# Six layer norms of a pass split into two halves of two tiles, in a two-slot FP32 model on one core

## The chip, the cores and the metric

One core of a Trainium2 chip runs the whole program. The metric is the device time of one execution in microseconds. The engines are TensorE (PE; its weight loads are PEld), VectorE (DVE), ScalarE (ACT), GpSimd (POOL) and SyncE (SP), each with an instruction queue of its own that it works off in order. They wait for each other only by semaphores.

## The reference

A four-layer stack over `x` (64 batches x 64 tokens x 128 features) with a context (64 x 128 x 128): cross-attentions with 16 and 8 heads, a recurrent layer, mixtures of experts, linear, softmax and local attention, and a state-space layer. What matters here is the norm without weights that stands ahead of every block. The kernel takes the mean out of it through centred weight matrices, so that on the tokens only the multiply by 1/sqrt(v + eps) is left:

```python
def _layernorm(x, axis=-1, eps=1e-05):
    m = jnp.mean(x, axis=axis, keepdims=True)
    v = jnp.var(x, axis=axis, keepdims=True)
    return (x - m) / jnp.sqrt(v + eps)
...
    x = x + _L0_attn_ref(_layernorm(x, axis=-1), L0_attn_W_hg, L0_attn_W_out)
...
    x = x + _L1_xattn_ref(_layernorm(x, axis=-1), ctx_1024, L1_xattn_Wq, L1_xattn_bq, L1_xattn_Wk, L1_xattn_bk, L1_xattn_Wv, L1_xattn_bv)
    x = x + _L1_attn_ref(_layernorm(x, axis=-1), L1_attn_wqkv, L1_attn_wo)
...
    x = x + _L2_attn_ref(_layernorm(x, axis=-1), L2_attn_w_qkv, L2_attn_b_qkv, L2_attn_w_out, L2_attn_b_out)
...
    x = x + _L3_attn_ref(_layernorm(x, axis=-1), L3_attn_w_in, L3_attn_conv_w, L3_attn_conv_b, L3_attn_w_B, L3_attn_w_C, L3_attn_w_out)
    x = x + _L3_ffn_ref(_layernorm(x, axis=-1), L3_ffn_Wg, L3_ffn_bg, L3_ffn_W1, L3_ffn_b1, L3_ffn_W2, L3_ffn_b2)
```

These six calls are the norms `rnn`, `x1`, `lin`, `loc`, `ssm` and `m3` of the kernel.

## The kernel before

The 64 batches are worked in 4 passes of 2 slots; a slot holds 8 batches, that is 512 tokens as 4 tiles of 128 tokens (partitions) by 128 features. The two slots are two independent programs with buffers of their own (`X_0`, `X_1`, `P_0`, `ps_0` and so on), and every engine interleaves them: each engine's program is a Python generator per slot, a `yield` ends a segment, and `weave` takes the next segment from slot 0 or 1 by one bit of a long number in `ORDER` (2496 segments on TensorE, 2038 on VectorE, 610 on GpSimd). So the order on each engine is written out beforehand, and an engine stands wherever its next segment waits for a semaphore, whatever else would be ready.

A norm is a chain over three engines and back. The names here are those of six norms per pass: `rnn`, `x1`, `lin`, `loc`, `ssm`, `m3`, so 48 in all. VectorE adds a block's result to the residual `X` (four L1456 instructions of one tile each, or one L1438, L1447 of all four tiles), takes `bn_stats` of four tiles (L1358), `bn_aggr` of four tiles (L1363), adds epsilon for all four in one instruction (L1378, for `loc` L1694) and signals `var`. GpSimd raises 128x4 variances to the power -0.5 (L1851) and signals `rstd`. VectorE multiplies the four tiles, 128x512, by it (L1373, `P<-X,small`) and signals `tok`. TensorE turns the four tiles (L457, four transposes, `ps<-cst,P`), and ScalarE copies them out (L1087), upon which the block's matmuls begin. L1373 is also used for norms that the change leaves alone (`P<-P`, `P<-Z`, `ctok<-ctok`). Within VectorE each step that reads the one before waits for the semaphore `chain` (`link`).

Beside the chain, GpSimd multiplies the attention probabilities of the other slot (L1878), products of the gated experts (L1968), and context tiles of 128x1024 (L1888, L1892).

Of the kernel before, what the change touches and what calls it, by code (L numbers as in the profile page):

```python
# [13 lines left out]
D = 128  # L14
# [45 lines left out]
def offsets(table):  # L60
    at, out = 0, {}
    for name, n in table:
# [14 lines left out]
    pe=(2496, int(""  # L77
        "4120180e82000011000000000033dbffdf375f56bac10c1af4ddee629cc55cb06914148810afbdc018a1ca1dd3aea84c3e9c"
        "718588ed73ea800018bfd2ff8eeff53ec40001008e1d720e74051814070f83ff8382011c3a86cb5fd6febfbbc1c3fc3f6bec"
        "ccfc9476f7fbd7dee707114148a0a7def5401651c3ac0c754163eb71c58b2c5ae72000031bf767ff15fde3dc4a0c3e0ebb82"  # L80
        "246bffffc0003902b06a40100000e439f3ff8b6fd6eeffdff647fc30abfa6ee58a2955ed703911029140530ef3d502c48e0e"
        "baea85bfff7b7be0b144aacd402003e97fd1f15d1f4000129ddea1b801158affffe1a82e00e20000000896b8ff7faeb75f5f"
        "fc1860ae9bffefeffc1f85bf2f38ca502505053d3ced401660e33f2d482affffffffe07ffbdffffeefc192d91eeb2a041812"
        "dfb1ff19e1d41389fff30f", 16)),
    act=(1740, int(""
        "4401061400110000000337bffe4faf4fbbecfa82c43130cc0901c000424af78f68bde1856031e6e0e18fee19bfff58103014"
        "e974e32054b018c306405ee0ccfddff73fffee99f10e8fbf7be8b0cc090382010ab95a0f687de350c30cdaa00f1fecc9bffd"
        "d21ccbfaed022dbf00068fb40010001773393fdefffde7fefeef1a24256470cc024118020224f0efcd3fffb35f0081ed5070"
        "fa7f80df9800ecf5fc310055f1e58ff000000009cf3e7bbf67ffbb7ff5ff13e03e6e06c0840e02010cb62fe641bffffff5ff"
        "f4ffff5838af0bfd2213de037fa0178ff", 16)),  # L90
    dve=(2038, int(""
        "51c7388080000c0000007fdaef5f0ec569738a609769cf6c61853036fc5b143437e800f1a3a936bb996fc30e0c0ca2361f15"
        "7ef2dcdbdbb07d80514d3c18ec83bd80000620488fb961e400a5ff9c78fe3e7186a7f643cfffe78f03cfc5b1593fc3b5011d"
        "294e78078efc30e483c818c7c0d7bf35db6adf0bffef3703473b19000ad95848c200001f0081b5eebbbdeff07fc74975ccd7"
        "318648e83cfc3a16341a1b8b68a33294e77377e5fe8cf019946305faf5ddc0db283de6ef3038032e7e306dc5801800000e37"
        "0022eddcb9ffc441aa4fffeb5fe9e1ce79e037d928b46fc9e5011e88ce7b1913fbffffe1fffcffffe4f1b19c78c77f000eb3"
        "67fd", 16)),
    pool=(610, int(""
        "673400df30532b53182161b93a2fbb7378c7904c253ac34fc0ff53185609d43957dee378c7cb219c0e0dee3a2b53142131b5"
        "3af57f8db607c0b9807706bc935fa660ac0ae49ffff3be7d1d", 16)),  # L100
# [4 lines left out]
def weave(program, order):  # L105
# [5 lines left out]
    for k in range(count - 1, -1, -1):  # L111
# [11 lines left out]
          "x3.r", "ssm", "m3", "m3.oh", "x0"]  # L123
TURNS = ["lat", "rnn", "lora", "lora.c", "x1", "lin", "lin.y", "m1", "m1.y", "rms", "x2.c0", "x2.c1", "x2",
# [9 lines left out]
MANY = {"kv": KV, "var": VARS, "rstd": VARS, "tok": TOKENS, "zT_ps": TURNS, "zT": COPIES, "y_ps": SUMS, "x_biased": BIASED,  # L134
# [21 lines left out]
def build(nc, x, ctxin, ctok_in, fold, cols, weights, consts, out):  # L156
# [4 lines left out]
    with stack:  # L161
# [71 lines left out]
        def by_tile(ap):  # L233
            return ap.rearrange("p (t d) -> p t d", d=D)
# [157 lines left out]
        with nc.Block() as block:  # L392
# [61 lines left out]
            def _(pe):  # L454
# [4 lines left out]

                def turn_onehot(s, i, name, k):  # L460
# [212 lines left out]
                def rnn(s, i):  # L673
# [9 lines left out]
                    yield  # L683
                    pe.wait_ge(*on("tok", s, i, "rnn"))
                    turn(s, 0, N[s])
# [34 lines left out]

                def cross(s, i):
                    yield
                    pe.wait_ge(*on("tok", s, i, "x1"))
                    turn(s, 0, N[s])
                    yield
                    pe.wait_ge(*on("zT", s, i, "x1"))
# [1391 lines left out]
```

## Time and profile before

| | us |
|---|---|
| median of 3 runs | 2501.07 (2498.35 to 2501.4) |
| the profiled execution, its own time | 2500.71 |
| its span in the trace | 2498.9 |
| TensorE busy | 2348.2 (94%) |
| VectorE busy | 1479.4 (59%) |
| ScalarE busy | 1179.5 (47%) |
| GpSimd busy | 930.1 (37%) |

Busy time is the union of an engine's instruction durations; what is left of the span is idle. TensorE has 150.7 us of it. The number behind a wait's arrow is the idle time of an engine just before an instruction, and the arrow names the instruction whose signal ended it.

### The profile page before, as it was taken

How to read it: one execution, taken by the hardware profiler on the slowest of the kernel's cores; microseconds unless marked ns; L12 is line 12 of the kernel's file. 1: busy time of each engine (PE TensorE's matmuls, PEld its weight loads, DVE VectorE, ACT ScalarE, POOL GpSimd, SP SyncE). 2: the span in 40 equal slices, each digit the busy share in tenths (PEclk: the TensorE clock that was granted, in tenths of full speed). 3: DMA queues.
4: the chain of work that ended last, by engine and by line, in shares of the span. 5: the costliest groups of instructions: out<-in, count | busy, mean ns of one | idle time of the engine just before them, and what ended most of it. 6: DMA issues, size and time to landing. Idle time of an engine off the chain costs nothing.

```text
span 2498.9 us, 41865 instructions
## 1 busy us (share of the span) xinstructions
PE 2348.2 (94%) x16412; PEld 1565.1 (63%) x16412; DVE 1479.4 (59%) x4008; ACT 1179.5 (47%) x2994; POOL 930.1 (37%) x853
## 2 busy tenths in 40 slices
PE   8999999999999999999999999999999999999998
PEld 5666665656756665665666666566566666656665
DVE  5457566665575666665564566665565555764653
ACT  4554334455444534445554454445455435354543
POOL 5334253533233335434232344543322343544400
PEclk8999999999999999999999999999999999999999
DMA  5000000000000000000000000000000000000000
GB/s 232 1 1 2 1 9 6 14 1 18 1 1 10 1 1 10 9 10 9 9 1 9 1 1 9 1 9 10 13 1 1 5 1 1 1 1 1 1 1 9
DMA packets 6676, 26.56 MB, mean 11 GB/s; under 512 B 848, under 2 KB 848, under 8 KB 5840
## 3 DMA queue, kind: packets, MB, share of 16 engines
q1 hardware_dynamic: 6480, 23.89, 2.6%
q8 instruction: 130, 2.13, 0.4%
q14 instruction: 66, 0.54, 0.1%
HBM read 21.79 MB, written 2.10 MB: 10 GB/s over the span
## 4 chain that ended last, share of the span: by engine, by line
PE 71%; DVE 17%; ACT 4%; POOL 4%; issue 3%; DMA 0%; SPq 0%; DVEq 0%; POOLq 0%; ACTq 0%
PE ps L472 10%; PE ps L485 7%; PE ps L529 6%; PE ps L504 6%; PE ps L866 4%; PE ps L606 3%; PE ps L496 3%; PE ps L583 3%; PE ps L457 3%; PE ps L576 3%; PE ps L628 2%; PE ps L581 2%; PE ps L823 2%; PE ps L813 2%; PE ps L655 2%
## 5 line engine op out<-in xcount | busy, mean ns | idle before, releaser
L1878 POOL TENSOR_TENSOR P<-P,small 128x384 f32<-128x384 f32 x384 | 317.3, 849 | 551.5 <-DVE small L1398 551.0
L1112 ACT ACTIVATE P<-ps,small 128x192 f32<-128x192 f32 x768 | 314.3, 421 | 154.9 <-DVE small L1390 153.3
L1851 POOL TENSOR_TENSOR small<-small,mhalf 128x4 f32<-128x4 f32 x112 | 129.0, 1151 | 554.0 <-DVE small L1378 317.0
L485 PE MATMUL ps<-kvT,big 128*128 128x192 f32 x1536 | 314.3, 335 | 6.8 <-DVE big L1405 2.5
L485 PEld LDWEIGHTS ps<-kvT,big 128*128 128x128 f32 x1536 | 248.6, 191 | 89.2 <-issue 52.1
L1390 DVE TENSOR_REDUCE small<-ps 128x2 f32<-128x384 f32 x384 | 210.1, 551 | 107.9 <-PE ps L485 100.5
L472 PEld LDWEIGHTS ps<-wts,P 128*128 128x128 f32 x1920 | 231.5, 192 | 43.8 <-issue 30.0
L472 PE MATMUL ps<-wts,P 128*128 128x128 f32 x1920 | 249.0, 279 | 5.2 <-POOL P L1968 2.6
L1968 POOL TENSOR_TENSOR P<-T 128x512 f32<-128x512 f32 x96 | 126.6, 1319 | 206.6 <-ACT T L1259 107.7
L504 PEld LDWEIGHTS ps<-value,big 128*128 128x128 f32 x1536 | 178.2, 192 | 25.8 <-issue 20.4
L504 PE MATMUL ps<-value,big 128*128 128x128 f32 x1536 | 188.2, 278 | 0.0
L529 PE MATMUL ps<-kvT,score 128*128 128x512 f32 x384 | 181.1, 613 | 6.5 <-ACT kvT L1087 5.0
L496 PE MATMUL ps<-cst,P 128*128 128x128 f32 x1152 | 166.4, 278 | 18.5 <-POOL P L1878 9.0
L496 PEld LDWEIGHTS ps<-cst,P 128*128 128x128 f32 x1152 | 132.3, 143 | 50.2 <-issue 18.2
L1112 ACT ACTIVATION_READ_ACCUMULATOR P<-ps,small 128x1 f32 x768 | 157.0, 204 | 0.0
L1285 ACT ACTIVATE P<-ps,col 128x512 f32<-128x512 f32 x128 | 81.3, 684 | 132.6 <-PE ps L870 132.5
L606 PEld LDWEIGHTS ps<-Vbd,P 128*64 128x64 f32 x3072 | 98.0, 139 | 53.5 <-issue 31.8
L372 POOL TENSOR_TENSOR big<-big,cst 128x1024 f32<-128x1024 f32 x48 | 106.5, 2222 | 65.2 <-ACT big L1277 37.8
L1456 DVE SCALAR_TENSOR_TENSOR X<-ps,small,X 128x128 f32<-128x128 f32 x256 | 71.9, 343 | 99.4 <-PE ps L472 94.0
L529 PEld LDWEIGHTS ps<-kvT,score 128*128 128x128 f32 x384 | 70.3, 194 | 84.5 <-issue 74.3
L1595 DVE TENSOR_REDUCE small<-ps 128x8 f32<-128x512 f32 x128 | 87.6, 685 | 58.4 <-PE ps L628 58.2
L1129 ACT ACTIVATE big<-ps 128x512 f32<-128x512 f32 x96 | 57.3, 597 | 133.0 <-PE ps L496 132.7
(281 smaller groups left out, 4476.0 us busy)
## 6 DMA issues: line engine op xcount, KB each, us to landing
ctok<-ctok_dram SPq DMA_DIRECT2D x8, 512.0 KB, 3.7
ctxT<-ctx_dram SPq DMA_DIRECT2D x8, 512.0 KB, 3.6
wts<-weights_dram SPq DMA_DIRECT2D x1, 2530.0 KB, 24.1
wts<-weights_dram SPq DMA_DIRECT2D x1, 2189.0 KB, 17.8
X<-x_dram SPq DMA_DIRECT2D x8, 256.0 KB, 3.4
big<-fold_dram SPq DMA_DIRECT2D x2, 1024.0 KB, 9.1
out_dram<-X SPq DMA_DIRECT2D x8, 256.0 KB, 2.0
wts<-weights_dram SPq DMA_DIRECT2D x1, 1536.0 KB, 26.7
```

Of the source, the lines that this page charges most:

```text
L372: return engine.tensor_tensor(big[s][:, 1024 * (t % 2):1024 * (t % 2) + 1024].rearrange("p (b j t) -> p b j t", b=2, t=SEQ), src[:, 128 * ...
L472: m = pe.matmul(part(s, k, t), tile_of(src, t), w, start=first and t == 0 and c == 0, stop=last and t == TILES - 1 and c == len(pairs) - 1)
L485: m = pe.matmul(ps[s][:, at:at + KEYS], big[s][:, BANK * b + 128 * p:BANK * b + 128 * p + 128], kvT[s][:, keys_at(b):keys_at(b) + KEYS], s ...
L496: m = pe.transpose(part(s, k, p), probs(s, j)[:, PAIR * p + at:PAIR * p + at + 128], C("ident"))
L504: m = pe.matmul(part(s, 1, t), big[s][:, 1024 * t + 128 * k:1024 * t + 128 * k + 128], value[:, at:at + 128], start=(t == 0 and k == 0), s ...
L529: m = pe.matmul(bank(s, qp_bank(g, r) + k), score[:, 128 * block_of(h, nh):128 * block_of(h, nh) + 128], latents(s), start=True, stop=True)
L606: m = pe.matmul(ps[s][64 * bb:64 * bb + 64, at:at + 18], src(bb, j), Vbd[s][:, 18 * (8 * b + j):18 * (8 * b + j) + 18], start=True, stop=True)
L1112: m = act.activation(probs(s, b // 2)[:, to:to + KEYS], ps[s][:, at:at + KEYS], ACT.Exp, bias=small[s][:, 4 * e + p:4 * e + p + 1], accum_ ...
L1390: dve.tensor_reduce(small[s][:, at:at + 2], ps[s][:, BANK * k:BANK * k + 2 * KEYS].rearrange("p (c k) -> p c k", k=KEYS), AX.X, ALU.max, n ...
L1851: pool.tensor_tensor(rstd(s, name, n), variance(s, name, n), mhalf[:, 0:n], ALU.pow).then_inc(*sig("rstd", s))
L1878: m = pool.tensor_tensor(view, view, over(small[s][:, at:at + 2], 2, [128, 2, KEYS]), ALU.mult)
L1968: pool.tensor_tensor(P[s][:, 1024 + 512 * (k % 2):1536 + 512 * (k % 2)], tmp(s, k % 2), tmp(s, 2 + k % 2), ALU.mult)\
```

## The change

For the six norms the work of four tiles is cut into two halves of two tiles. VectorE takes `bn_stats` of tiles 0, 1 and 2, aggregates 0 and 1, takes `bn_stats` of tile 3, adds epsilon for tiles 0 and 1 and signals `var` a first time, then aggregates 2 and 3, adds epsilon and signals a second time. GpSimd does two powers of 128x2, VectorE two multiplies of 128x256, TensorE two pairs of transposes, each behind its own wait. The signal to ScalarE (`zT_ps`) comes after the second pair, as before after the fourth transpose, and ScalarE's copy and all that follows is the same. Matmuls, transposes and their shapes are the same in number. `ORDER` has new numbers for every engine but SyncE.

```diff
 ORDER = dict(
-    pe=(2496, int(""
-        "4120180e82000011000000000033dbffdf375f56bac10c1af4ddee629cc55cb06914148810afbdc018a1ca1dd3aea84c3e9c"
...
+    pe=(2544, int(""
+        "8088190ca078016400000000008cf3dff7b78abafb858d0d5f4edd05c51578c88a0c445069f7bea5b073a75c54160000f938"
...
+                def turn_halves(s, i, name, k, src):
+                    for h in range(2):
+                        yield
+                        pe.wait_ge(*on("tok", s, i, name if h else name + ".0"))
+                        for t in (2 * h, 2 * h + 1):
+                            m = pe.transpose(part(s, k, t), tile_of(src, t), C("ident"))
+                    m.then_inc(*sig("zT_ps", s))
...
                 def cross(s, i):
-                    yield
-                    pe.wait_ge(*on("tok", s, i, "x1"))
-                    turn(s, 0, N[s])
+                    yield from turn_halves(s, i, "x1", 0, N[s])
...
+                    stats(0)
+                    first = mark(stats(1))
+                    stats(2)
+                    dve.wait_ge(chain, first)
+                    aggregate(0)
+                    first = mark(aggregate(1))
+                    second = mark(stats(3))
+                    dve.wait_ge(chain, first)
+                    plus_eps(0)
+                    dve.wait_ge(chain, second)
+                    aggregate(2)
+                    link(aggregate(3))
+                    plus_eps(1)
+
+                def rescale_halves(s, i, name, dst, src):
+                    for h in range(2):
+                        yield
+                        dve.wait_ge(*on("rstd", s, i, name if h else name + ".0"))
+                        dve.tensor_tensor(by_tile(dst)[:, 2 * h:2 * h + 2, :], by_tile(src)[:, 2 * h:2 * h + 2, :],
+                                          over(rstd(s, name)[:, 2 * h:2 * h + 2], 2, [128, 2, D]), ALU.mult).then_inc(*sig("tok", s))
...
-                    yield from norm(s, i, "x1", res(s, i), N[s], weights_centred=True)
+                    yield from norm_halves(s, i, "x1")
...
+                def inverse_root_halves(s, i, name):
+                    for h in range(2):
+                        yield
+                        pool.wait_ge(*on("var", s, i, name if h else name + ".0"))
+                        pool.tensor_tensor(rstd(s, name)[:, 2 * h:2 * h + 2], variance(s, name)[:, 2 * h:2 * h + 2], mhalf[:, 0:2], ALU.pow)\
+                            .then_inc(*sig("rstd", s))
```

What the orders show at three places. The line numbers after the change are those of the new file: 472 are the transposes of a half, 487, 832 and 822 what 472, 823 and 813 were, 1909 what 1860 was, 2017 what 1968 was.

TensorE in pass 0, between the last matmuls of slot 1's `lora` block (`ps_1<-wts,T_1`) and the transposes of its norm `x1`; before:

```order
L472 MATMUL ps_1<-wts,T_1 128x128 x3
L823 MATMUL ps_0<-A_0,wts 128x512 [waits m1_t0,m1_ab0]
L813 MATMUL ps_0<-A_0,wts 128x512
L472 MATMUL ps_0<-wts,P_0 128x128 [waits m1_g0]
L472 MATMUL ps_0<-wts,P_0 128x128 x3
L823 MATMUL ps_0<-A_0,wts 128x512 [waits m1_t0,m1_ab0]
L813 MATMUL ps_0<-A_0,wts 128x512
L457 MATMUL ps_1<-cst,P_1 128x128 [waits tok1]
L457 MATMUL ps_1<-cst,P_1 128x128 x3
```

and after:

```order
L487 MATMUL ps_1<-wts,T_1 128x128 x3
L832 MATMUL ps_0<-A_0,wts 128x512 [waits m1_t0,m1_ab0]
L822 MATMUL ps_0<-A_0,wts 128x512
L487 MATMUL ps_0<-wts,P_0 128x128 [waits m1_acc0,m1_g0]
L487 MATMUL ps_0<-wts,P_0 128x128 x3
L832 MATMUL ps_0<-A_0,wts 128x512 [waits m1_t0,m1_ab0]
L822 MATMUL ps_0<-A_0,wts 128x512
L472 MATMUL ps_1<-cst,P_1 128x128 [waits tok1]
L472 MATMUL ps_1<-cst,P_1 128x128
L472 MATMUL ps_1<-cst,P_1 128x128 [waits tok1]
L472 MATMUL ps_1<-cst,P_1 128x128
```

The same eight matmuls of slot 0 (four of 512 columns, four of 128; the trace has two records of each FP32 matmul) lie ahead of the transposes; the second pair stands directly behind the first.

TensorE in pass 2, between slot 0's state-space output (`ps_0<-wts,P_0`) and the transposes of its norm `m3`; before:

```order
L472 MATMUL ps_0<-wts,P_0 128x128 x7
L581 MATMUL ps_1<-big_1,T_1 128x512 [waits pT_act1]
L583 MATMUL ps_1<-A_1,T_1 128x512
L584 MATMUL ps_1<-A_1,T_1 128x512
L504 MATMUL ps_1<-value2,big_1 128x128 [waits exped1]
L504 MATMUL ps_1<-value2,big_1 128x128 x7
L496 MATMUL ps_1<-cst,P_1 128x128 [waits p_ready1,mix_dve1,mix_act1]
L496 MATMUL ps_1<-cst,P_1 128x128 x3
L457 MATMUL ps_0<-cst,P_0 128x128 [waits tok0]
L457 MATMUL ps_0<-cst,P_0 128x128 x3
```

and after:

```order
L487 MATMUL ps_0<-wts,P_0 128x128 x7
L519 MATMUL ps_1<-value2,big_1 128x128 [waits exped1]
L519 MATMUL ps_1<-value2,big_1 128x128 x7
L511 MATMUL ps_1<-cst,P_1 128x128 [waits p_ready1,mix_dve1,mix_act1]
L511 MATMUL ps_1<-cst,P_1 128x128 x3
L511 MATMUL ps_1<-cst,P_1 128x128 [waits p_ready1]
L511 MATMUL ps_1<-cst,P_1 128x128 x3
L472 MATMUL ps_0<-cst,P_0 128x128 [waits tok0]
L472 MATMUL ps_0<-cst,P_0 128x128
L511 MATMUL ps_1<-cst,P_1 128x128 [waits pT_act1]
L511 MATMUL ps_1<-cst,P_1 128x128 x3
L472 MATMUL ps_0<-cst,P_0 128x128 [waits tok0]
```

Less of slot 1 lies ahead of the norm's transposes than before (the mixing matmuls L581 to L584 went ahead of slot 0's output), and four transposes of slot 1 lie between the two pairs.

VectorE in pass 0 at the norm `x1` of slot 1, from `bn_stats` on. Before, with its last step:

```order
L1358 BN_STATS small_1<-X_1_0 128x6 x3
L1363 BN_AGGR small_1<-small_1 128x2 [waits chain]
L1363 BN_AGGR small_1<-small_1 128x2 x3
L1378 TENSOR_SCALAR small_1<-small_1 128x4 [waits chain]
L1675 SCALAR_TENSOR_TENSOR T_0<-P_0,ps_0 128x512 [waits m1_g0,m1_t0]
L1373 TENSOR_TENSOR P_1<-X_1_0,small_1 128x512 [waits rstd1]
```

and after:

```order
L1383 BN_STATS small_1<-X_1_0 128x6 x2
L1386 BN_AGGR small_1<-small_1 128x2 [waits chain]
L1386 BN_AGGR small_1<-small_1 128x2
L1383 BN_STATS small_1<-X_1_0 128x6
L1389 TENSOR_SCALAR small_1<-small_1 128x2 [waits chain]
L1386 BN_AGGR small_1<-small_1 128x2 [waits chain]
L1386 BN_AGGR small_1<-small_1 128x2
L1389 TENSOR_SCALAR small_1<-small_1 128x2 [waits chain]
L1410 TENSOR_TENSOR P_1<-X_1_0,small_1 128x256 [waits rstd1] x2
L1718 SCALAR_TENSOR_TENSOR T_0<-P_0,ps_0 128x512 [waits m1_g0,m1_t0] x2
```

The experts' product of slot 0, which stood between epsilon and the multiply, now stands behind both multiplies.

## Rows read from the trace of the kernel before

**Rows 1.** The page's busy times, granted TensorE clock, and chain by engine.

```profile
PE 2348.2 (94%) x16412; PEld 1565.1 (63%) x16412; DVE 1479.4 (59%) x4008; ACT 1179.5 (47%) x2994; POOL 930.1 (37%) x853
...
PEclk8999999999999999999999999999999999999999
...
PE 71%; DVE 17%; ACT 4%; POOL 4%; issue 3%; DMA 0%; SPq 0%; DVEq 0%; POOLq 0%; ACTq 0%
```

**Rows 2.** TensorE's waits over the span: us in total, times, longest.

```profile
PE ps L457 <- DVE P L1373: 30.9, 42, 2.9
PE ps L496 <- POOL P L1878: 9.0, 14, 2.2
PE ps L472 <- DVE big L1470: 7.4, 5, 2.6
```

**Rows 3.** Timeline, norm `x1`, slot 1, pass 0: start, duration, engine, line, idle before.

```profile
309.09 0.87 DVE L1358 BATCH_NORM_STATS2 small<-X 128x6 f32<-128x128 f32 x4
...
309.37 1.05 PE L472 MATMUL ps<-wts,P 128*128 128x128 f32 x8
...
310.26 1.02 PE L823 MATMUL ps<-A,wts 128*128 128x512 f32 x2
...
311.12 1.02 PE L813 MATMUL ps<-A,wts 128*128 128x512 f32 x2
...
312.56 0.66 PE L457 MATMUL ps<-cst,P 128*128 128x128 f32 x4 [0.42 <-DVE P L1373]
```

**Rows 4.** Timeline, norm `ssm`, slot 1, pass 3, with nothing beside the chain.

```profile
2440.03 0.86 DVE L1358 BATCH_NORM_STATS2 small<-X 128x6 f32<-128x128 f32 x4
...
2440.93 0.38 DVE L1363 BATCH_NORM_AGGREGATE small<-small 128x2 f32<-128x6 f32 x4
2441.34 0.17 DVE L1378 TENSOR_SCALAR small<-small 128x4 f32<-128x4 f32 x1
2441.59 1.01 POOL L1851 TENSOR_TENSOR small<-small,mhalf 128x4 f32<-128x4 f32 x1 [4.40 <-DVE small L1378]
2442.63 0.69 DVE L1373 TENSOR_TENSOR P<-X,small 128x512 f32<-128x512 f32 x1 [1.12 <-POOL small L1851]
...
2443.38 0.66 PE L457 MATMUL ps<-cst,P 128*128 128x128 f32 x4 [1.16 <-DVE P L1373]
```

**Rows 5.** Timeline of TensorE, pass 3: the last of the 25 waits counted.

```profile
2450.37 0.66 PE L457 MATMUL ps<-cst,P 128*128 128x128 f32 x4 [0.25 <-DVE P L1373]
```

**Rows 6.** Groups by line and shape of GpSimd: shape, count, busy us, mean ns, idle before.

```profile
L1851 POOL TENSOR_TENSOR small<-small,mhalf 128x4 f32<-128x4 f32 x112 | 129.0, 1151 | 554.0 <-DVE small L1378 317.0 <-DVE small L1480 165.5 <-DVE small L1694 37.4
...
L1892 POOL TENSOR_TENSOR T<-T,col 128x1024 f32<-128x1024 f32 x16 | 34.7, 2166 | 1.2
...
L1892 POOL TENSOR_TENSOR T<-T,col 128x512 f32<-128x512 f32 x16 | 17.5, 1093 | 1.1
...
L1948 POOL TENSOR_TENSOR small<-small,mhalf 128x4 f32<-128x4 f32 x8 | 8.0, 1003 | 0.0
...
L1997 POOL MEMSET A<- 128x8 f32 x8 | 0.9, 114 | 0.0
```

**Rows 7.** Groups by line and shape of VectorE, same columns.

```profile
L1373 DVE TENSOR_TENSOR P<-X,small 128x512 f32<-128x512 f32 x48 | 48.4, 1008 | 22.4 <-POOL small L1851 22.1
...
L1585 DVE TENSOR_TENSOR kvT<-ps,small 128x128 f32<-128x128 f32 x96 | 27.9, 291 | 3.3
```

**Rows 8.** Timeline, pass 1: `m3` of slot 0 beside a GpSimd multiply.

```profile
1152.34 2.00 POOL L1888 TENSOR_TENSOR T<-ctok,col 128x1024 f32<-128x1024 f32 x1
...
1152.41 2.48 DVE L1373 TENSOR_TENSOR P<-X,small 128x512 f32<-128x512 f32 x1
...
1154.94 0.78 PE L457 MATMUL ps<-cst,P 128*128 128x128 f32 x4 [1.42 <-DVE P L1373]
```

**Rows 9.** Timeline, pass 2: a power on GpSimd, and a VectorE multiply beside it.

```profile
1450.33 1.01 POOL L1948 TENSOR_TENSOR small<-small,mhalf 128x4 f32<-128x4 f32 x1
...
1450.40 0.69 DVE L1373 TENSOR_TENSOR P<-Z,small 128x512 f32<-128x512 f32 x1 [0.31 <-POOL small L1851]
```

More of the change, by code:

```diff
@@ L123, with halves @@
           "x3.r", "ssm", "m3", "m3.oh", "x0"]
+HALVED = ["rnn", "x1", "lin", "loc", "ssm", "m3"]
+def halves(names):
+    return [m for n in names for m in ([n + ".0", n] if n in HALVED else [n])]
 TURNS = ["lat", "rnn", "lora", "lora.c", "x1", "lin", "lin.y", "m1", "m1.y", "rms", "x2.c0", "x2.c1", "x2",
@@ L1459, in rnn @@
                 def rnn(s, i):
-                    yield from norm(s, i, "rnn", res(s, i), N[s], weights_centred=True)
+                    yield from norm_halves(s, i, "rnn")
                     yield
@@ L1609, in linear @@
                 def linear(s, i):
-                    yield from norm(s, i, "lin", res(s, i), N[s], weights_centred=True)
+                    yield from norm_halves(s, i, "lin")
                     yield
@@ L1692, in local @@
                     yield
-                    moments(s, "loc", res(s, i))
-                    dve.tensor_scalar(variance(s, "loc"), mean_var(s, "loc")[:, :, 1], EPS5, None, ALU.add).then_inc(*sig("var", s))
+                    moments_halves(s, "loc", res(s, i))
                     link(dve.tensor_reduce(small[s][:, MEAN:MEAN + 8], ctxT[s][:, :].rearrange("p (b k) -> p b k", k=CTX), AX.X, ALU.add))
@@ L1697, in local @@
                        .then_inc(*sig("x3_sum", s))
-                    yield from rescale(s, i, "loc", N[s], res(s, i))
+                    yield from rescale_halves(s, i, "loc", N[s], res(s, i))
                     yield
@@ L1762, in ssm @@
                 def ssm(s, i):
-                    yield from norm(s, i, "ssm", res(s, i), N[s], weights_centred=True)
+                    yield from norm_halves(s, i, "ssm")
                     yield
@@ L1792, in moe3 @@
                 def moe3(s, i):
-                    yield from norm(s, i, "m3", res(s, i), N[s], weights_centred=True)
+                    yield from norm_halves(s, i, "m3")
                     yield
@@ L1925, in program @@
                         yield from heads(s, i, 1)
-                        yield from inverse_root(s, i, "rnn")
+                        yield from inverse_root_halves(s, i, "rnn")
                         yield
@@ L1978, in program @@
                         yield from heads(s, i, 2)
-                        yield from inverse_root(s, i, "loc")
+                        yield from inverse_root_halves(s, i, "loc")
                         yield
@@ L1992, in program @@
                         yield from inverse_root(s, i, "x3")
-                        yield from inverse_root(s, i, "ssm")
+                        yield from inverse_root_halves(s, i, "ssm")
                         yield
```

88 lines of the change are left out of this document (46 added, 42 removed).

## The prediction

> **What bounds the kernel now.** I read the page's busy times first, then TensorE's waits, then the timeline at single norms. TensorE is busy 2348.2 of 2498.9 us, and the chain that ended last runs 71% over TensorE and 17% over VectorE [rows 1]. The order changes no matmul, and the granted clock stands at 9 tenths or more in all slices after the first [rows 1]. So what can be won lies in TensorE's 150.7 us of idle time, and what can be lost is added to it. The largest single entry there is the wait of the transposes for the norm's multiply on VectorE: 30.9 us in 42 waits; the next, for the normalised probabilities, is 9.0 us [rows 2]. No other engine is near its limit (59%, 47%, 37%), so their own work counts only where TensorE waits for it.
>
> The 30.9 us aren't all of the six norms. Matching the 42 waits with the norms, in the order in which they stand on TensorE, 25 belong to the six norms, from 0.42 us at 312.56 [rows 3] to 0.25 us at 2450.37 [rows 5]; they add to 17.2 us. The other 17 waits, 13.7 us, are at norms that stay whole. At 23 of the 48 changed norms TensorE doesn't wait at all, since enough work of the other slot lies ahead.
>
> **The chain before.** Where nothing disturbs it [rows 4], from the first statistic: VectorE's moments end at 1.48 us, the power runs from 1.56 to 2.57, the multiply from 2.60 to 3.29, TensorE starts at 3.35. Four transposes at a spacing of 0.12 us (0.66 less the last one's 0.27 or so of latency, over three) end the chain at about 3.84 of TensorE's time.
>
> **The change, part by part.** *Statistics on VectorE.* Four of them span 0.86 us, four aggregates 0.38 [rows 4], so three statistics, two aggregates, one more statistic and an epsilon of 0.17 give the first `var` at about 1.2 us. Two aggregates and a second epsilon follow; the second `var` comes at about 1.5, as the only one did. The added instruction falls in time that was spent on `chain` waits.
>
> *The power.* The trace has no 128x2 power. Four columns take 1.00 us (1003 ns undisturbed; the mean of 1151 holds cases lengthened by a running VectorE multiply, [rows 6]), and two directly behind each other aren't faster (the second has no idle time before it and still takes 1003). Half of it is bounded from above by 1.00, if the cost belongs to the instruction. From below: a small memset of 8 columns takes 0.11, which I take as the fixed part, and half of the rest gives 0.56. GpSimd's multiplies speak for the lower end: 512 columns take 1093 ns, 1024 take 2166 [rows 6], twice as much, with next to nothing fixed. I take 0.60. Then the first power runs 1.28 to 1.88, the second 1.88 to 2.48 (by then the second `var` has been there for long). With 1.00 it would be 1.28 to 2.28 and 2.28 to 3.28.
>
> *The multiplies.* 128x512 takes 0.69 us undisturbed [rows 4], 128x128 takes 0.29 [rows 7]; in between, 256 columns take 0.42. The second runs 2.52 to 2.94, and TensorE can start its second pair at about 3.0, which ends at 3.24. That is 0.60 us earlier than 3.84. The first multiply, 1.92 to 2.34, lies wholly under the second power.
>
> Does GpSimd's power hold that first multiply up? A VectorE multiply that starts 0.07 us behind a power takes 0.69 us, as without one [rows 9], and there are six such cases. A GpSimd multiply does hold it: one of 2.00 us that began 0.07 us ahead made the same VectorE instruction 2.48 us long [rows 8], and the mean of 1008 ns over the 48 holds 16 longer ones [rows 7]. The Trainium skill ("GPSIMD Engine Reference", Specifications) says that GpSimd's interfaces to SBUF are shared with VectorE, with contention for VectorE instructions that have two inputs in SBUF; the trace agrees for GpSimd's multiplies, not for its powers. By that rule the first multiply would wait for the end of the second power; what this gives is a rival below.
>
> *The gain on TensorE.* Take from each of the 25 waits what the chain gains, 0.60 us, or the wait itself where it is shorter: summed over the 25 that is 11.1 us. Where a GpSimd multiply holds the second half as in [rows 8], the same amount comes from its earlier start, the shorter remainder and the two transposes that are already done. With a gain of 0.30 us it would be 6.8, with 0.80 it would be 12.7.
>
> *Added work.* 48 more epsilons of 0.17 us [rows 4] and 48 more fixed parts of a multiply (0.29 for 128 columns and 0.69 for 512 leave 0.16 at zero) are 16 us on VectorE, 1% of its busy time. Of TensorE's idle time some 80 us end on VectorE (the 30.9 and 7.4 of [rows 2] are the largest of it), 0.05 us for each us that VectorE is busy, so 16 us cost about 1. GpSimd gets 48 times 0.20, 10 us, ahead of the other slot's probabilities in its queue; the 9.0 us of waits for those [rows 2], over 930 us busy, give 0.1. Then 48 more waits on TensorE: 0.02 us each by the spacing of transposes with and without a wait, 1 us. Sum 2.
>
> *The new order.* It is the part that can't be priced by one row. Between the last matmul of a block and the transposes of the next norm, TensorE's cover is the other slot's work. At `x1` of slot 1 in pass 0 it is 4.48 us: two stretches of L823 and L813 of 1.77 and a stretch of 0.94, by the distances of their starts [rows 3]. The wait was 0.42, so 4.90 us are needed. The change keeps that cover. But over the 40 norms other than `rnn` the sums of cover go from 39.5 to 33.9 us for `x1`, 41.7 to 37.7 for `lin`, 59.6 to 53.3 for `loc`, 42.1 to 30.3 for `m3`, and from 47.6 to 58.6 for `ssm`; and 40 of 48 second pairs stand directly behind the first, so that the second half decides. The order spends part of the shorter chain on turning earlier. What it gains by that elsewhere I take as nothing, because the cover of all other waits must grow by what these lose, 16.7 us net, and nothing in the profile says whether it falls on waits or on stretches already covered. Ends: 0 and -12.
>
> Sum: -11 for the waits, +2 for added work, 0 for the order: -9 us of 2500.7, 0.36%. The median of the runs is 0.4 us above the profiled execution, so about 2492.
>
> **The rivals.** *The power costs the same for two columns as for four (slower).* For: 1003 ns for four columns is some hundred times what a multiply takes for a column (2.1 ns), so it may be mostly a fixed routine. Against: GpSimd's other costs go with columns. The place is GpSimd, between the two powers. With a half of p the second pair could start at 1.28 + 2p + 0.52 and end 0.24 later, so the chain is as long as before at p = 0.90, and beyond it longer: at 1.00 by 0.2 us. By the covers, need 4.90 (4.47 where one 0.69 us add precedes, `m3` and `loc`), the shortfall over the 40 norms is 10.7 us in the order of before, 11.3 in that of after at p = 0.60, 15.9 at 0.75 and 27.8 at 1.00. So it would be 17.1 slower and 2 of added work: about 2520. VectorE then also stands twice for a power (42 of the 48 pairs of multiplies are next to each other on it), with the experts' products and maxima of the other slot queued behind.
>
> *The shortfall only moves (no change).* The same count says that at p = 0.60 waits at the norms stay where they are, 11.3 for 10.7 us, because the order has cut the cover by as much as the chain. Then the gain must come from what runs earlier behind the transposes; if that is covered already, or ends on ScalarE's copies, +0.6 and +2 give 2504.
>
> *The order pays in both.* The 16.7 us of cover moved elsewhere fall on waits, worth up to 12: about 2480.
>
> *The power holds the first multiply.* Then both multiplies come after the second power; the first ends 0.42 late but the second only some 0.3, the chain gains 0.3, the 25 waits give about 6: 2497, no change by the bound below. Against it stand the six cases [rows 9].
>
> **How the numbers follow.** About 0.2%, 5 us, is what a measurement of this kernel can tell from no change. Forecast 2492: 0.41. Order pays more, 2480: 0.15. Shortfall moves, 2504: 0.22. First multiply held, 2497: 0.05. Power fixed, 2520: 0.17. So faster 0.56, within 0.2% 0.27, slower 0.17. The range runs from 2478 (the order's case) to 2512, which takes in a half power of up to about 0.85 (by the count 9.7 us more at the norms, and 2) and leaves out most of the fixed one.
>
> **What would show it.** GpSimd's 128x2 power at 0.55 to 0.65 us confirms the chief step; 0.9 or more refutes it. The multiply of 256 columns at 0.42, its first one not lengthened under the second power. TensorE's wait for the norm's multiply should fall from 30.9 to about 20 us, its idle time from 151 to about 142 us, with busy time the same. If that wait stays near 30 while others fell, the order has spent the gain elsewhere, and total idle time tells whether it paid. Waits for normalised probabilities well above 9.0 us would mean that GpSimd's added powers matter. The forecast is wrong if total idle doesn't fall though the chain got shorter.

## The result, and the profile after

| | us |
|---|---|
| before, median of 4 runs | 2500.68 (2498.35 to 2501.4) |
| after, median of 4 runs | 2519.74 (2517.53 to 2521.23) |
| ratio | 1.0083, 95% interval 1.0069 to 1.0097 |
| span after, in the trace | 2519.4 |
| TensorE busy / idle after | 2364.9 / 154.5 |

The change makes the kernel 19 us slower by the medians, 0.76%. The ratio in the table isn't the quotient of the two medians; its interval is 17 to 24 us. The forecast was 2492 with 2512 as the upper end. The page after, busy times, granted clock in tenths and chain by engine, to be held against [rows 1]:

```profile
PE 2364.9 (94%) x16412; PEld 1570.2 (62%) x16412; DVE 1499.7 (60%) x4104; ACT 1175.6 (47%) x2994; POOL 940.2 (37%) x901
...
PEclk8999999999999999999999999999999999999999
...
PE 70%; DVE 18%; ACT 5%; POOL 4%; issue 2%; DMA 0%; SPq 0%; DVEq 0%; POOLq 0%; ACTq 0%
```

Two things are to be seen. TensorE has the same 16412 records of matmuls as before, yet is busy 16.7 us longer (2364.9 against 2348.2), while its idle time grew by only 3.8. And the row of the granted clock reads the same as before: a digit there covers 63 us and can't show what happened. The list of cores has the mean, after:

```profile
core 0: 2519.4 us, clock 0.983
```

Before it was 0.988. TensorE's waits after, for [rows 2]:

```profile
PE ps L472 <- DVE P L1410: 27.7, 40, 2.0
PE ps L464 <- DVE P L1379: 13.7, 14, 2.3
PE ps L511 <- POOL P L1927: 8.2, 12, 2.1
```

L472 are the transposes of the six norms' halves, L464 those of the norms that stay whole; before, both stood on L457 (30.9 us, 17.2 of it at the six). So the six norms' own waits went up, from 17.2 to 27.7 us, where the forecast had them fall by 11. The power and the multiply of a half, by their lines (min, median, max in ns):

```profile
L1899 POOL TENSOR_TENSOR small<-small,mhalf x96: 694/697/716, 136.9 to 2492.3; 128x2 f32<-128x2 f32 x96
...
L1410 DVE TENSOR_TENSOR P<-X,small x96: 393/425/2219, 137.7 to 2493.0; 128x256 f32<-128x256 f32 x96
```

The power of two columns takes 0.697 us, not 0.60. The multiply takes 0.42 as forecast, but some take up to 2.2.

**Where busy time grows.** The timeline after at `m3` of slot 0 in pass 1, the norm of [rows 8] (start, duration, engine, line; of a 512-column matmul the trace has two records, "x2", while the transposes have one each):

```profile
1169.12 1.36 POOL L1899 TENSOR_TENSOR small<-small,mhalf 128x2 f32<-128x2 f32 x2 [9.46 <-DVE small L1389]
1169.27 1.02 PE L591 MATMUL ps<-big,T 128*128 128x512 f32 x2
...
1169.85 0.43 DVE L1410 TENSOR_TENSOR P<-X,small 128x256 f32<-128x256 f32 x1 [0.39 <-POOL small L1899]
1170.34 0.44 PE L472 MATMUL ps<-cst,P 128*128 128x128 f32 x2
1170.45 2.00 POOL L1937 TENSOR_TENSOR T<-ctok,col 128x1024 f32<-128x1024 f32 x1
1170.52 2.21 DVE L1410 TENSOR_TENSOR P<-X,small 128x256 f32<-128x256 f32 x1 [0.24 <-POOL small L1899]
...
1172.79 0.44 PE L472 MATMUL ps<-cst,P 128*128 128x128 f32 x2 [2.01 <-DVE P L1410]
1173.06 1.85 PE L596 MATMUL ps<-big,T 128*128 128x512 f32 x2
```

The first multiply lies under the second power and takes 0.43 us. The second starts 0.07 us behind a GpSimd multiply and takes 2.21, as the whole one did in [rows 8]; TensorE waits 2.01 us for it. Then comes a 512-column matmul that takes 1.85 us; one of the same size took 1.02 just before the gap (L591). TensorE by stretches (length, busy per engine, granted clock in the third column from the end):

```profile
1170.00:1172.50 2.50, 0.73 (x3) 0.20 (x2) 2.26 (x2) 0.00 (x0) 2.45 (x2) 1.00 0.00 0
1173.00:1175.00 2.00, 2.00 (x6) 0.50 (x4) 0.00 (x0) 0.60 (x1) 1.59 (x1) 0.53 0.00 0
1177.00:1179.00 2.00, 2.00 (x10) 1.29 (x11) 1.65 (x14) 0.44 (x1) 0.00 (x0) 1.00 0.00 0
```

After the gap the granted clock is 0.53 though TensorE is busy all of the 2 us: that is the 1.2 GHz level (the rest is the edge of the stretch). At 1177 it is back at 2.4 GHz. So this gap is paid for twice, once as idle time and once as slow matmuls. The same thing happened in the kernel before at the same norm: behind the wait of 1.42 us at 1154.94 [rows 8] its stretch reads

```profile
1154.90:1159.40 4.50, 4.46 (x14) 2.53 (x14) 1.27 (x4) 2.32 (x9) 3.98 (x4) 0.62 0.00 0
```

**The sum over the kernel.** From the trace's clock records I added the time at the lower level, in stretches that begin behind the first 20 us and end before TensorE's work does: 44.4 us in 11 stretches before, 68.3 us in 16 after. A matmul takes nearly twice as long there (1.85 us against 1.02), so about half of that time is lost, and 23.9 us more of it make 12 of the 16.7 us of added busy time; the other 4.7 aren't explained. This and all later "half-clock" times are such sums of mine.

A pause alone doesn't make the clock fall. Behind the first 20 us TensorE pauses 40 times for 0.94 us or more in the kernel before, and 40 times after. Within the 5 us ahead of every one of the 11 stretches before stands such a pause, and ahead of 14 of the 16 after; most of the 40 have no fall behind them. What sets apart those that have isn't shown here.

The Trainium skill ("TensorE: Matmul & The Clock Gate", section "HAM oscillation — how this bites in real kernels") tells of kernels whose TensorE idles for data between groups of matmuls and starts each next group at half clock, at the price of half the throttled time. The trace agrees, with VectorE in place of the DMA as the one that is waited for: 0.53 behind the gap above, and half of the half-clock time in the sum over kernels further down. It doesn't agree in that each group would start so: 29 of the 40 long pauses before have no fall behind them.

### The profile page after: what moved, and what is told of

Read it like the earlier page. It is cut to its first block, busy times and chain, and to the rows that moved or that the text cites. A ratio compares the mean times of both kernels' runs of the same rounds, so it can differ in the third digit from the quotient of the medians.

```text
span 2519.4 us, 42000 instructions
## 1 busy us (share of the span) xinstructions
PE 2364.9 (94%) x16412; PEld 1570.2 (62%) x16412; DVE 1499.7 (60%) x4104; ACT 1175.6 (47%) x2994; POOL 940.2 (37%) x901
## 4 chain that ended last, share of the span: by engine, by line
PE 70%; DVE 18%; ACT 5%; POOL 4%; issue 2%; DMA 0%; SPq 0%; DVEq 0%; POOLq 0%; ACTq 0%
PE ps L487 10%; PE ps L500 6%; PE ps L544 6%; PE ps L519 6%; PE ps L873 4%; PE ps L621 3%; PE ps L511 3%; PE ps L598 3%; PE ps L591 3%; PE ps L643 3%; PE ps L596 3%; PE ps L832 2%; PE ps L822 2%; PE ps L464 2%; ACT P L1115 2%
## 5 line engine op out<-in xcount | busy, mean ns | idle before, releaser
L1893 POOL TENSOR_TENSOR small<-small,mhalf 128x4 f32<-128x4 f32 x64 | 79.9, 1248 | 267.8 <-DVE small L1523 179.3
L1899 POOL TENSOR_TENSOR small<-small,mhalf 128x2 f32<-128x2 f32 x96 | 66.0, 701 | 270.9 <-DVE small L1389 269.8
```

## The experiments

Times are medians, ratios are to the kernel before in the same session.

**1. The halves in the order of before.** `ORDER` is that of before; both halves stand in one segment:

```diff
                 def turn_halves(s, i, name, k, src):
+                    yield
                     for h in range(2):
-                        yield
                         pe.wait_ge(*on("tok", s, i, name if h else name + ".0"))
```

and the same in `rescale_halves` and `inverse_root_halves`.

> The halves of all six norms, in the order of before: the second half of each engine's work stands in the same segment as the first, so the numbers of ORDER are those of the kernel before. Theory A (the new order is the cause: it gives the norm's chain less cover, TensorE stands there more, and its granted clock falls more often): with the measured 0.70 us for a power of 128x2 the chain is 0.40 us shorter than before, the 25 waits give min(wait, 0.40) = 8.6 us, 2 us go for added work, so about 2494 us, TensorE's wait for the norm's multiply near 22 us, half-clock time near that of before (44 us behind the start). Theory B (the halves themselves cost more than they give, by 48 more powers and VectorE standing twice): 2515 to 2520 us as in the changed kernel, wait for the norm's multiply 27 us or more.

Measured: 2496.6 us, ratio 0.9985 [0.9975, 0.9995]. The page's busy times of this kernel:

```profile
PE 2343.6 (94%) x16412; PEld 1559.8 (63%) x16412; DVE 1495.6 (60%) x4104; ACT 1179.0 (47%) x2994; POOL 943.2 (38%) x901
```

Its waits of the transposes of the halves, and its line in the list of cores:

```profile
PE ps L472 <- DVE P L1410: 15.4, 23, 1.7
```

```profile
core 0: 2493.6 us, clock 0.992
```

The halves by themselves don't slow the kernel; they gain 4 to 5 us (1 to 6 by the interval). But the six norms' waits fell only from 17.2 to 15.4. Half-clock time is 30.7 us.

**2. The order alone.** Before's work in after's order; the whole norm's work stands at the second half's place (an extra `yield` ahead of it on TensorE, VectorE and GpSimd):

```diff
+                def turn_late(s, i, name, k, src):
+                    yield
+                    yield
+                    pe.wait_ge(*on("tok", s, i, name))
+                    turn(s, k, src)
```

> Norms of four tiles as before, in the order of after: each engine does the whole of the norm's work where its second half stands. Theory A: as slow as the changed kernel or slower, since the chain is 0.40 us longer under the same short cover: 2520 to 2535 us. Theory B: back to about 2500 us, since the added powers and waits are gone.

Measured: 2532.12 us, ratio 1.0118 [1.0103, 1.0134]. Busy times from its page, then TensorE's wait for the multiply:

```profile
PE 2368.3 (94%) x16412; PEld 1576.0 (62%) x16412; DVE 1483.7 (59%) x4008; ACT 1177.4 (47%) x2994; POOL 925.7 (37%) x853
```

```profile
PE ps L457 <- DVE P L1369: 49.0, 43, 2.8
```

The order costs 31 us with whole norms, and 23 us with halves (2519.7 against 2496.6). The halves are worth 12 us by the medians in this order, 9 by the ratios, and 4 to 5 in the old one. Half-clock time is 85.3 us, idle time 162.4.

**3. Cut only behind the power.** Experiment 1 with one epsilon and one 128x4 power; multiply and transposes stay cut.

```diff
-                        yield from inverse_root_halves(s, i, "rnn")
+                        yield from inverse_root(s, i, "rnn")
...
-                        dve.wait_ge(*on("rstd", s, i, name if h else name + ".0"))
+                        dve.wait_ge(*on("rstd", s, i, name))
```

> Order of before; one epsilon and one power of 128x4 per norm as before, only the multiply and the transposes are cut in two. The chain is some 0.2 us shorter than before (0.24 for the two transposes done ahead, less the fixed part of the second multiply). Theory A: the waits shorten by up to 0.2 us each, about 4 us, less 1 us: 2497 to 2499 us. Theory B: if it is the cut itself that costs (VectorE standing, TensorE's second wait), 2505 us or more.

Measured: 2516.95 us, ratio 1.0063 [1.0049, 1.0077]; the wait for L1389, here the multiply, is 24.4 us in 27. The multiply's own line (ns min, median, max):

```profile
L1389 DVE TENSOR_TENSOR P<-X,small x96: 411/424/2217, 130.7 to 2480.9; 128x256 f32<-128x256 f32 x96
```

This is the surprise: in the good order, cutting the multiply without cutting the power costs 16 us against before. Counting multiplies that took over 0.5 us (over 0.75 for whole ones): before 14 of 48, with 14.5 us above that bound; here 28 of 96, 14 first and 14 second halves, with 32.1 us; in experiment 1 22 of 96, 7 first and 15 second, with 21.6 us. Every one of these long multiplies overlaps a GpSimd multiply, none a power alone. With a single power GpSimd is free as soon as it ends and may begin its next multiply, and then either half can be caught. With two powers the second one keeps GpSimd from a multiply while VectorE does the first half. That GpSimd holds the halves is seen in the durations; that it is the whole of the 16 us isn't shown. Half-clock time is 61.4 us.

**4 and 5. No power,** in after and in before: the powers of the six norms are replaced by a product of two constants, so these two kernels leave out the factor 1/sqrt(v + eps).

```diff
-                        pool.tensor_tensor(rstd(s, name)[:, 2 * h:2 * h + 2], variance(s, name)[:, 2 * h:2 * h + 2], mhalf[:, 0:2], ALU.pow)\
+                        pool.tensor_tensor(rstd(s, name)[:, 2 * h:2 * h + 2], mhalf[:, 4:6], mhalf[:, 0:2], ALU.mult)\
```

> The changed kernel with the powers of the six norms replaced by a GpSimd multiply of two constants of the same shape, 128x2 (so the output is not that of the reference): the same instructions and waits, with about 0.1 us in place of 0.70. The chain gets some 1.2 us shorter. Theory A predicts that the new order works well with a short chain: 2490 us or less, wait for the norm's multiply under 12 us. If the new order is bad in other places, it stays above 2505 us.

Measured: 2509.86 us, ratio 1.0037 [1.0022, 1.0053].

> The kernel before with the powers of the six norms replaced by a GpSimd multiply of two constants of the same shape, 128x4 (so the output is not that of the reference). The chain is 0.9 us shorter with the order of before. Theory A: waits at the six norms fall from 17 to about 6 us and the time to 2480 to 2488 us; the new order with as short a chain gave 2510 us, so that the difference of some 25 us is the order's own, whatever the chain costs. Rival (the new order is only worse because it counts on a shorter chain): 2500 us or more.

Measured: 2486.47 us, ratio 0.9949 [0.9934, 0.9964]; its waits for the norm's multiply:

```profile
PE ps L457 <- DVE P L1373: 23.7, 36, 2.6
```

Even with the power nearly free the new order is slower than before, so the price of a two-column power isn't what made the change slower. In the old order a chain that is shorter by some 0.85 us is worth 13 us (2499.4 to 2486.5); the six norms' waits fall from 17.2 to 10.4. The six waits give only 6.8 of the 13 us; TensorE's idle time as a whole falls by 8.8. The difference between the orders is again 23 us.

**6. The context's multiplies behind the multiply of `m3`.** Experiment 1, and GpSimd waits:

```diff
                         pool.wait_ge(*on("ssm_g", s, i))
+                        pool.wait_ge(*on("tok", s, i, "m3"))
```

> The halves in the order of before, as in the run with that order, and one wait more: GpSimd's two multiplies of the next pass's context (128x1024) also wait for the signal of the whole norm m3. In the run without it VectorE's 96 multiplies of 128x256 hold 22 that are longer than 0.5 us, 21.6 us in excess, since a GpSimd multiply was running, and TensorE waits 6.7 us at m3. Theory H (GpSimd's multiply holds VectorE's, and that is where m3's waits come from): waits at m3 fall to 2 us or less and the time by 3 to 8 us, to about 2490 us. Rival: GpSimd's context multiplies come too late for what waits on them, and the time stays or rises.

Measured: 2494.96 us, ratio 0.9977 [0.9967, 0.9987]. Busy times from its page, then TensorE's wait for the halves:

```profile
PE 2350.7 (94%) x16412; PEld 1565.1 (63%) x16412; DVE 1481.2 (59%) x4104; ACT 1178.3 (47%) x2994; POOL 942.5 (38%) x901
```

```profile
PE ps L472 <- DVE P L1410: 10.1, 18, 1.5
```

The holds at `m3` go: VectorE is busy 14 us less than in experiment 1 with the same 4104 instructions, and the waits at `m3` fall from 6.8 to 1.5 us. The six norms' waits are now 10.1 us, 7.1 below before's, 4.0 of them at `m3`, where before had holds of its own. Part of it comes back elsewhere: the waits for normalised probabilities rise from 8.2 to

```profile
PE ps L511 <- POOL P L1927: 11.7, 16, 2.4
```

The time is lower by 1.6 us only, which the intervals don't tell from nothing. In this trace idle time is 5.4 us lower than in experiment 1 and half-clock time 17.1 us higher (47.8 against 30.7), but it was the execution with the lowest mean clock of the kernel's 11.

**7 to 9. The clock taken out.** Ahead of the wait for a norm's multiply TensorE does transposes that nobody reads, at the places where it waits long (187, 232 and 205 of them in experiment 1's kernel, in after and in before):

```diff
                     for h in range(2):
+                        fill(s, i, name, h)
                         pe.wait_ge(*on("tok", s, i, name if h else name + ".0"))
...
+                def fill(s, i, name, h=0):
+                    for _ in range(FILL.get((i, name, s, h), 0)):
+                        pe.transpose(part(s, FILL_BANK[name], 3), tile_of(W("w1"), 0), C("ident"))
```

> The halves in the order of before, with 187 transposes more on TensorE whose results nobody reads, placed right ahead of the waits of the norms' transposes, so many at each of 33 waits as fit in the gap the trace shows there (about 23 us in all). Theory C (the granted clock of TensorE falls behind stretches in which it stands, and each us at half clock costs half a us of work): the half-clock time behind the start, 31 us, falls to 15 us or less and the time by 5 to 8 us. Rival: the clock does not follow the gaps; the added work delays what follows a little, 0 to 5 us slower.

Measured: 2490.31 us, ratio 0.9968 [0.9956, 0.998]; half-clock time 20.5 us. From its list of cores:

```profile
core 0: 2487.4 us, clock 0.994
```

> The changed kernel with 232 transposes more on TensorE whose results nobody reads, in the gaps ahead of 34 waits of norms' transposes (about 29 us in all). Theory C: half-clock time falls from 68 us to 30 us or less, so the time from 2519.7 to about 2500 us. Rival: 2520 to 2525 us. What is left over 2496.6 us (the same halves in the order of before) would be the order's idle time alone.

Measured: 2503.81 us, ratio 1.0018 [1.0009, 1.0027]; half-clock time 23.9 us. At the norm shown above, the timeline of this kernel reads

```profile
1165.08 2.21 DVE L1457 TENSOR_TENSOR P<-X,small 128x256 f32<-128x256 f32 x1 [0.24 <-POOL small L1946]
1165.17 1.80 PE L515 MATMUL ps<-cst,wts 128*128 128x128 f32 x15
...
1167.35 0.44 PE L510 MATMUL ps<-cst,P 128*128 128x128 f32 x2 [0.38 <-DVE P L1457]
1167.63 1.02 PE L638 MATMUL ps<-big,T 128*128 128x512 f32 x2
```

and a stretch of 2 us behind the held multiply, and the line of the list of cores

```profile
1168.00:1170.00 2.00, 2.00 (x10) 0.66 (x8) 0.24 (x1) 0.67 (x2) 1.15 (x1) 1.00 0.00 0
```

```profile
core 0: 2503.2 us, clock 0.992
```

The multiply is held as before (2.21 us), the transposes L510 start no earlier in relation to it, but the fifteen unread ones (L515) stand in the gap and the next 512-column matmul takes 1.02 us instead of 1.85. Such filling, over the kernel, takes 16 us off after.

> The kernel before, with nothing of the change, and 205 unread transposes in TensorE's gaps at 35 waits of norms. Theory C (stretches at half clock follow gaps): half-clock time from 44 us to under 20 us, time from 2500 to about 2490 us. Then the filling is worth as much without the halves as with them, and against the halves with filling (2490.3 us) it tells what the halves are worth where the clock is out of it: by the idle time 3 to 6 us.

Measured: 2490.05 us, ratio 0.9966 [0.9954, 0.9978]; half-clock time 13.7 us. Before and the halves in the old order are the same to 0.3 us once the gaps are filled. So the 4 to 5 us that the halves gain in experiment 1 are mostly time at half clock (44.4 us before, 30.7 there), not a shorter path. The table of all executions further down says the same.

**10. The cover restored.** In after, at six of the 48 norms (four of them `m3`, five in the last two passes) the second pair of transposes is put behind the next one or two segments of the other slot, 8 us of work in all; TensorE's numbers in `ORDER` alone change. It is a part of the lost cover, not all of it. As TensorE's order reads at one of these places (- after, + this kernel):

```diff
-L472 MATMUL ps<-cst,P 128x128 x4
 L596 MATMUL ps<-big,T 128x512
 L598 MATMUL ps<-Z,T 128x512
 L599 MATMUL ps<-Z,T 128x512
+L472 MATMUL ps<-cst,P 128x128 x4
```

> The changed kernel with six bits of TensorE's order exchanged: at six norms (five of them in the last two passes, four m3) where the count of covers says that the second pair of transposes comes too early for a chain with powers of 0.70 us, the pair now stands behind the next one or two segments of the other slot, 8 us of work moved ahead in all. Nothing else differs. Theory A (short cover at the norms is what makes the new order slow): the waits for the norm's multiply fall by 4 to 5 us from 27.7, with fewer stretches at half clock, and the time by 5 to 10 us, to 2510 to 2515 us. Rival (the loss is spread over the whole order): 2518 us or more.

Measured: 2518.7 us, ratio 1.0078 [1.0064, 1.0091]. Its wait of the halves:

```profile
PE ps L472 <- DVE P L1410: 21.2, 33, 1.6
```

The waits at the halves fall from 27.7 to 21.2 us, the idle time doesn't (155.7 against 154.5), and the time stays. So what these six places give comes back at other waits. That cover at the norms as a whole isn't the loss, this doesn't show: most of it stays as short as in after.

**11. Widths of the power,** in a single run: behind the last work GpSimd does powers and multiplies of 1, 2, 4 and 8 columns, twice each.

```diff
+                for w in (1, 2, 4, 8, 1, 2, 4, 8):
+                    for op in (ALU.pow, ALU.mult):
+                        pool.tensor_tensor(probe[:, at:at + w], stat(0, "m1", 32, w), mhalf[:, 0:w], op)
+                        at += w
```

> The kernel before, with 16 more GpSimd instructions at its start, ahead of its own work: a power and a multiply of 128x1, 128x2, 128x4 and 128x8, twice each, into a buffer of their own. From 1.007 us for 4 columns and 0.697 for 2, a power costs 0.39 us and 0.155 for a column if that is a line: 0.54, 0.70, 1.01, 1.63 us. If it is a fixed part and steps, 128x1 takes 0.70 like 128x2. The multiplies show what a small instruction costs at all: by 128x512 and 128x1024 next to nothing beyond 0.1 us.

The probes ran at the end of the program, at 2469 to 2478 us, not at its start. The line of the probes, powers and multiplies together:

```profile
L2022 POOL TENSOR_TENSOR probe<-small,mhalf x16: 183/414/1630, 2469.2 to 2477.9; 128x1 f32<-128x1 f32 x4, 128x2 f32<-128x2 f32 x4, 128x4 f32<-128x4 f32 x4, 128x8 f32<-128x8 f32 x4
```

One by one the powers took 0.55, 0.70, 1.00 and 1.63 us for 1, 2, 4 and 8 columns; the multiplies 0.19 at every width, but for the first of 0.28. So a power is about 0.39 us fixed and 0.155 for each column.

**12. What the findings give together.** Experiment 6's kernel with 151 unread transposes at 28 waits.

> Halves in the order of before, GpSimd's context multiplies behind norm m3, and 151 unread transposes in TensorE's gaps at 28 waits of norms. Parts measured so far: 2496.6 us without the last two, 2495.0 with the wait, 2490.3 with the filling. If the two add: about 2488 us, half-clock time at most 20 us. Rival (the filling already bought what the wait buys): 2490 us or more.

Measured: 2488.23 us, ratio 0.9949 [0.9936, 0.9962], clock 0.992, half-clock time 23.9 us. It is the fastest kernel here that does all of the computation, 12.5 us below before; its interval overlaps those of the filled kernels of 7 and 9, so the wait on GpSimd isn't shown to add to the filling.

**All traces side by side** (us; half-clock time without the first 20 us):

| kernel | span | busy | idle | half-clock | span - idle - half of half-clock |
|---|---|---|---|---|---|
| before | 2498.9 | 2348.2 | 150.7 | 44.4 | 2326.0 |
| after | 2519.4 | 2364.9 | 154.5 | 68.3 | 2330.8 |
| 1, halves, old order | 2493.6 | 2343.6 | 150.0 | 30.7 | 2328.2 |
| 2, whole, new order | 2530.6 | 2368.3 | 162.4 | 85.3 | 2325.6 |
| 3, cut behind the power | 2511.9 | 2358.1 | 153.8 | 61.4 | 2327.4 |
| 4, no power, new order | 2504.4 | 2358.0 | 146.4 | 54.6 | 2330.7 |
| 5, no power, old order | 2486.1 | 2344.2 | 141.9 | 41.0 | 2323.7 |
| 6, context behind `m3` | 2495.3 | 2350.7 | 144.6 | 47.8 | 2326.8 |
| 10, cover restored | 2515.9 | 2360.2 | 155.7 | 58.0 | 2331.2 |

The last column is nearly the same, 2323.7 to 2331.2, while the spans differ by 44 us: idle time and half the time at the lower clock are what these kernels differ in. Between the orders the second term moves more: from experiment 1 to after, idle time adds 4.5 us and the clock 18.8, of 25.8. Where the chain alone gets shorter, from before to experiment 5, it is the first: 8.8 us of idle time against 1.7.

Each row is one execution, and the clock differs from one to the next. Span and mean clock are known of every execution; the span times what its mean clock lacks of 1 is what the clock cost in it, the start included. Averages, in us:

| kernel | executions | cost of the clock | rest of the span |
|---|---|---|---|
| before, in the session of experiment 1 | 18 | 27.6 | 2470.9 |
| 1, halves, old order | 11 | 23.1 | 2472.0 |
| after | 4 | 39.7 | 2478.1 |
| 6, context behind `m3` | 11 | 26.1 | 2465.8 |
| 7, 1 filled | 6 | 16.2 | 2472.8 |
| 8, after filled | 11 | 18.9 | 2483.1 |

By these averages the halves in the old order gain nothing but clock. Of what after loses against before, 12 us are clock and 7 the rest; of what it loses against experiment 1, 17 and 6.

## Why the prediction was wrong, step by step

**"The granted clock stands at 9 tenths or more in all slices after the first."** This step failed, and with it the way in which everything was priced. The row was read rightly but is too coarse: 44.4 us at half clock, worth 22 us, were already in the kernel before, and are a few per cent of any slice. From it came "what can be lost is added to the idle time". In fact a gap of a microsecond or two can cost as much again in the matmuls behind it. Of after's 16.7 us of growth in busy time, 12 are that. The line that would have warned stood in the rows themselves: four transposes take 0.66 us in [rows 3, 4] and 0.78 behind the held multiply in [rows 8].

**"What it gains by that elsewhere I take as nothing ... Ends: 0 and -12."** This is the term that put the forecast outside its range; it failed in sign and size: it measures +23 us with halves, +31 with whole norms, +23 without powers. The prediction counted that cover at `x1`, `lin`, `loc` and `m3` shrinks and let the sum stand at nothing because cover elsewhere must grow. It gave the unknown term no end on the slow side, though a count of lost cover (16.7 us net) was at hand as such an end, and so the range couldn't hold the result. Where in the order the loss sits isn't settled: 8 us of cover restored at six norms (experiment 10) didn't change the time, and at equal progress of TensorE after lies 7 us behind experiment 1's kernel at 20%, 1 at 40%, 12.7 at 50%, 20 at 65% and 25 to 30 from 70% on, so it isn't one place. To give one engine the new order and leave the others theirs wasn't tried. With gaps filled the difference between the orders is 13.5 us (2503.81 against 2490.31), so about 10 of the 23 go with filling; but the unread transposes cost time of their own, in after 5 us of the rest of the span (2478.1 to 2483.1). By the averages over all executions 17 of the 23 are clock. The clock's share thus lies between 10 and 17; what makes up the others isn't shown.

**"I take 0.60" for half of the power.** Mis-sized: 0.697. The line from a memset of 0.11 us to the 1.00 of four columns went through the wrong fixed part; it is 0.39. By the prediction's own formula, 1.28 + 2p + 0.52 + 0.24, the chain then ends at 3.43 and not at 3.24, against 3.84: 0.41 us shorter, not 0.60. The range of 0.56 to 1.00 held it.

**"Take from each of the 25 waits ... 0.60 us, or the wait itself": -11.1.** Failed even in the old order, where nothing else moves: the six norms' waits fell by 1.8 us, and the time by 4 to 5. Two reasons are seen. The gain is 0.41, and more multiplies were held by GpSimd: 22 for 21.6 us against 14 for 14.5, so that the waits at `m3` rose from 5.5 to 6.8 us. With the holds at `m3` gone (experiment 6) the six norms' waits are 7.1 us below before's, but there before's own holds are gone too. How much of the missing gain each of the two reasons takes isn't shown. The prediction took it that a held second half still gains its earlier start; it didn't count that two multiplies can be caught where one was, and by other GpSimd multiplies than before. The prediction also held 16 of before's 48 multiplies to be lengthened; 14 are. Experiment 5, the power left out, looks like a success of the same reckoning, 13 us for some 0.85 where the prediction had 12.7 for 0.80, but it is luck in part: the six norms' waits fell by 6.8 us, and the other 6 came at other waits and through the clock, which the reckoning doesn't count.

**What was right.** The power doesn't hold the first multiply: in after 3 first halves and 18 second halves were held. The 256-column multiply takes 0.42. Added work on VectorE, GpSimd and TensorE was small: the kernel of experiment 1 got no slower for it. That VectorE's busy time rose there by the 16 us forecast (1479.4 to 1495.6) is luck, since about 8 of them are multiplies that GpSimd held longer; with the holds at `m3` gone it is 1481.2. Waits for normalised probabilities stayed (8.2 against 9.0).

**The rivals.** The time landed on the number of the rival in which the power costs the same for two columns as for four, 2520, but not for its reason: the power is 0.70, and without it the new order is still at 2509.86. The case "shortfall only moves" came nearest in kind, an order that takes back what the chain gives, but had the norms' waits stay where they are and priced it at 2504; they rose by 10.5 us. Its opposite, that the order pays, is refuted, and so is the held first multiply. The sign of being wrong that the prediction set itself, total idle time, did show (154.5, where 150.7 was before and 142 forecast), but by itself it would have called the result a small loss; four fifths of the loss (16.7 of 20.5 us of span) stood in busy time, which it had declared constant.

## What to carry to other kernels

Count the time at the lower clock in the trace before pricing an edit to an engine that is 94% busy: here a constant plus idle time plus half of the half-clock time gave every unfilled kernel's span to 4 us, and idle time alone didn't. Take it from several executions, since one kernel's differ by as much as an edit gains. When an edit comes with a new order, run the edit in the old order first; the order here was worth five times the edit, with the other sign. Where gaps can't be closed, unread transposes in them bought 16 us in after, 9 to 11 in before and 4 to 6 with the halves in the old order, as much as the halves did or more.

## What the runs showed of the hardware that was not expected

A GpSimd power of f32 on 128 partitions has a fixed part of about 0.39 us and 0.155 us for each column (0.55, 0.70, 1.00, 1.63 us for 1, 2, 4, 8), while a GpSimd multiply of these widths takes 0.19 at all of them. A VectorE multiply of 256 columns beside such a power takes 0.42 us, beside a GpSimd multiply of 1024 columns that began 0.07 us ahead 2.21 us, ending 0.28 us behind it. The other way round, 41 of the 112 powers of 128x4 in the kernel before took 1.32 to 1.51 us in place of 1.01; all 41 began while a VectorE instruction on two tensors was running. TensorE dropped to 1.2 GHz behind waits of 1.42 us (before) and 2.01 us (after) at one norm, though it was 94% busy over the kernel: 11 such stretches before, 16 after, 4 in before with its gaps filled, with as many long pauses (40) before as after. One kernel's own runs differ with it: before ran from 2491.86 us at a mean clock of 0.992 to 2505.32 at 0.988.
